# A transformer layer on one core: GpSimd's cost in the planner, head layout, fillers and the closing halves

## The chip, the cores and the metric

The kernel runs on one core of one Trainium2 chip. The metric is the device time of the whole program in microseconds (us); less is better. Five engines work from queues of their own, each strictly in its order: TensorE (PE, with its weight loads shown apart as PEld), VectorE (DVE), ScalarE (ACT), GpSimd (POOL) and SyncE (SP), which only issues transfers. They wait for each other on semaphores.

## The reference, cut to what matters

```python
xn = layernorm(x)                                  # x: 1 x 2048 x 128, f32
q, k, v = split(xn @ w_attn + b_attn)              # 16 heads of 8
scores = q @ k.T * 8 ** -0.5 + mask                # mask: -log(1 + delta) for keys AFTER the query, -inf before it
attn = softmax(scores) @ v
ffn = fp4(silu(fp4(xn) @ fp4(w_gate).T) * (fp4(xn) @ fp4(w_up).T)) @ fp4(w_down).T   # 352 wide
out = x + attn @ w_proj + b_proj + ffn
```

`fp4` quantizes blocks of 16 numbers and multiplies back. A query looks at itself and at the keys after it. Because the mask is minus a logarithm, exp(score + mask) = exp(score) / (1 + delta): the kernel multiplies the exponentials by a table of inverse distances, `dist`. This multiplication is called weighing here.

## The kernel before, in words

The 2048 queries are cut into four groups of 512 (`GROUPS = [3, 2, 0, 1]`) and the 16 heads into four quadruples. A group and a quadruple make a unit: 16 units. Each unit is walked twice. In the first walk (`max`) TensorE makes scores with queries on the partitions (L1425, with a triangle added at L1428) and VectorE takes the row maximum (L1240, 640 instructions). The maxima go back as three extra rows of the query operand, so that the second walk has them subtracted by the matmul itself. In the second walk (`st`), for each block of 128 keys and each head, TensorE makes the transposed scores (L1449, L1452), ScalarE the exponential (L1049), and then the exponentials are weighed and written into `ring`, eight slots of two heads each. A pair of heads is weighed either by GpSimd in one instruction over both heads (L895), after ScalarE has put the exponentials into the slot, or by VectorE in two instructions (L1267), which read PSUM and write the slot. A slot is `[P, GQ, 2]`: the two heads are interleaved, so VectorE writes every second number, and TensorE reads every second one. A step of four heads (two pairs) then goes through `pv` (L1467: the weighed values times V, four heads side by side on TensorE, accumulated in bank 7). There are 160 steps, 320 pairs, 640 heads. A slot is free again when the `pv` of its step is done, so `st` can be four steps ahead of `pv`.

After a unit's last step, ScalarE copies bank 7 out (`evac`, L1074), TensorE transposes it (`close`, L1475), and VectorE divides by the sums (`norm`, L1280 and L1281). After four units come a transpose (`turn`, L1483), ScalarE's copy with the bias (L1068), `project` (L1490), and VectorE's `add` into `xin` (L1292); SyncE stores the group (L795). The feed-forward part is cut into 16 tiles of 128 tokens and mixed in at fixed amounts of `st` work.

The order of every engine's queue is computed when the kernel is built, by `plan()`: a list scheduler that walks the four engines with a cost for each item. GpSimd's weighing costs `POOL_START + 2 * n * POOL_COL` there. The planner also decides, pair by pair, who weighs: VectorE if GpSimd's backlog, summed by the same cost, is above a bound.

```python
POOL_COL, POOL_START = 2.04, 220
POOL_QUEUE, LAST_QUEUE = 3800, 1500
behind = max(clock["POOL"], now) + waiting["POOL"] - now
pair_vec[p] = behind > (LAST_QUEUE if work["max"] == total else POOL_QUEUE)
```

`lead_at` says how far the maxima must be ahead of the second walk; VectorE puts a maximum ahead of a weighing only below that line. The same planner assigns the seven PSUM banks, and `bank_free_for` turns what held a bank before into a wait.

`FILL = 200` fillers (`warm`, L1310: a transpose of the identity into bank 7) have the lowest rank on TensorE and fill its gaps at the start. The first `pv`, which writes the same bank, is planned only after the last of them.

Of the kernel before, what the change touches and what calls it, by code (L numbers as in the profile page):

```python
# [12 lines left out]
P = 128  # L13
# [59 lines left out]
POOL_COL, POOL_START = 2.04, 220  # L73
# [4 lines left out]
def plan():  # L78
# [190 lines left out]
    bank_of, prior = {}, {}  # L269
    holder = [None] * BANKS  # L270
# [38 lines left out]
    def rank(engine, item, level, now):  # L309

        kind = item[0]
        if engine == "PE":
            free = len(free_banks(now))
            if kind in ("pv", "hT", "down", "warm"):
                return level
            if kind == "gu":
                return level if free >= 3 else None
            if kind == "max":
                ahead = issued["max"] - issued["maxed"]
                if ahead >= MAX_AHEAD or free < 2:  # L320
                    return None
                return 4 if ahead < 2 else 7
            if kind == "st":
                if issued["st"] - issued["exp"] >= EXP_AHEAD or issued["vec"] >= VEC_AHEAD or free < 2:
                    return None
                if item[1] // 2 >= SLOTS and ("PE", ("pv", (item[1] // 2 - SLOTS) // 2)) not in seen:
                    return None
                return 4.5
            return level if free >= 1 else None
        if engine == "DVE":  # L330
            if kind == "max":
                return 4 if work["max"] < lead_at(work["st"]) else 7
            if kind == "fp4" and item[2] == 2 and len(free_banks(now)) < HELD_FREE:
                return None
            return 5 if kind == "weigh" else level
        return level

    def take(engine, head, now):
# [7 lines left out]
        if engine == "PE" and kind not in ("pv", "hT", "down", "warm"):  # L346
            for o in [("gate", item[1]), ("up", item[1])] if kind == "gu" else [item]:
                b = min(free_banks(now), key=lambda k: (released(holder[k]) if holder[k] else 0, k))
                bank_of[o], prior[o], holder[b] = b, holder[b], o
# [6 lines left out]
        if engine == "ACT" and kind == "st":  # L356
# [62 lines left out]
    while True:  # L419
        busy = [e for e in queues if any(left[e].get(k, 0) < len(q) for k, q in queues[e].items())]  # L420
# [36 lines left out]
def build(nc, x, w_attn, b_attn, w_proj, b_proj, w_gate, w_up, w_down, out):  # L457
# [22 lines left out]
    with ExitStack() as ctx:  # L480
# [203 lines left out]

        def weights(d, n):
# [47 lines left out]
        def _(sp):  # L733
# [48 lines left out]
            for o in orders["SP"]:  # L782
# [8 lines left out]
                if o[0] == "out":  # L791
                    gi, g = o[1], GROUPS[o[1]]
                    sp.wait_ge(fin_ready, gi + 1)
                    sp.wait_ge(down_used, TPG * (gi + 1))
                    sp.dma_start(out_t[:, TPG * g:TPG * (g + 1), :],  # L795
                                 xin[:, TPG * g:TPG * (g + 1), :]).then_inc(stored, 16)
            sp.wait_ge(stored, 16 * NG)
# [123 lines left out]
        def _(act):  # L921
# [11 lines left out]
            for o in orders["ACT"]:  # L933
# [103 lines left out]
                if o[0] == "st":  # L1037
# [11 lines left out]
                    a_.activation(scores if pair_vec[p] else slot(p)[:, 0:n, e % 2], scores,  # L1049
# [11 lines left out]
                if o[0] == "turn":  # L1061
                    g = o[1]
                    act.wait_ge(attT_psum, g + 1)
# [4 lines left out]
                    a_.activation(attT, bank(*o), ACT.Identity, bias=bv[:]).then_inc(attT_ready, 1)  # L1068
                if o[0] == "evac":
# [4 lines left out]
                    a_.activation(osb[:, u % 2], psum[:, OUT_BANK, :], ACT.Identity).then_inc(o_ready, 1)  # L1074
# [3 lines left out]
        def _(vec):  # L1078
# [85 lines left out]
            for o in orders["DVE"]:  # L1164
# [93 lines left out]
                if o[0] == "weigh":  # L1258
# [8 lines left out]
                    v_.tensor_tensor(slot(p)[:, 0:n, e % 2], bank("st", e)[:, 0:n], weights(d, n),  # L1267
                                     ALU.mult).then_inc(weighed_vec, 1)
                if o[0] == "norm":
                    u = o[1]  # L1270
                    g, hq, _ = parts_of(u)
                    vec.wait_ge(oT_psum, u + 1)
                    if u >= NQ and hq == 0:
                        vec.wait_ge(attT_psum, u // NQ)
                    o4 = bank("close", u).rearrange("p (t j e) -> p t j e", t=TPG, j=4)
# [4 lines left out]
                    seq(v_.reciprocal(rz[:], o4[:, :, :, HD]))  # L1280
                    v_.tensor_tensor(att[:, :, 32 * hq:32 * hq + 32].rearrange("p t (j d) -> p t j d", d=HD),  # L1281
                                     o4[:, :, :, 0:HD],
                                     rz[:].rearrange("p t (j o) -> p t j o", o=1).to_broadcast([P, TPG, 4, HD]),
                                     ALU.mult).then_inc(att_ready, 1)
                if o[0] == "add":
                    g = GROUPS[o[1]]
                    res = xin[:, TPG * g:TPG * (g + 1), :]
                    vec.wait_ge(proj_psum, o[1] + 1)
                    if before(o, "sum") > 0:
                        vec.wait_ge(down_used, before(o, "sum"))  # L1290
                    projected = bank("project", o[1]).rearrange("p (t d) -> p t d", d=D)
                    v_.tensor_tensor(res, projected, res,  # L1292
                                     ALU.add).then_inc(fin_ready, 1)
# [3 lines left out]
        def _(pe):  # L1297
# [10 lines left out]
            for o in orders["PE"]:  # L1308
# [146 lines left out]
                if o[0] == "pv":  # L1455
# [9 lines left out]
                    for j in range(4):  # L1465
                        h = 4 * hq + j
                        ins = mm(psum[32 * j:32 * j + 32, OUT_BANK, 0:n], vaug[:, b, VC * h:VC * h + 32],  # L1467
                                 slot(2 * s + j // 2)[:, 0:n, j % 2], start=(b == NT - 1), stop=(b == TPG * g))
                    ins.then_inc(pv_done, 1)
                if o[0] == "close":  # L1470
                    u = o[1]
                    bank_free(*o)
                    pe.wait_ge(o_ready, u + 1)
                    for a in range(TPG):
                        ins = nc.tensor.transpose(bank(*o)[:, P * a:P * (a + 1)],  # L1475
                                                  osb[:, u % 2, P * a:P * (a + 1)], identf[:])
                    ins.then_inc(oT_psum, 1)
                if o[0] == "turn":
                    g = o[1]
                    bank_free(*o)  # L1480
                    pe.wait_ge(att_ready, 4 * g + 4)
                    for a in range(TPG):
                        ins = nc.tensor.transpose(bank(*o)[:, P * a:P * (a + 1)], att[:, a], identf[:])  # L1483
                    ins.then_inc(attT_psum, 1)
                if o[0] == "project":
                    g = o[1]
                    bank_free(*o)
                    pe.wait_ge(attT_ready, g + 1)
                    for a in range(TPG):
                        ins = mm(bank(*o)[:, P * a:P * (a + 1)], attT[:, P * a:P * (a + 1)], wp[:],  # L1490
                                 start=True, stop=True)
                    ins.then_inc(proj_psum, 1)
# [26 lines left out]
```

## Time and profile before

| | |
|---|---|
| median of 3 runs | 599.66 us (597.81 to 599.75) |
| the profiled execution: its time / its span | 599.36 us / 597.6 us |
| granted TensorE clock | 0.997 of full |
| TensorE, VectorE, GpSimd, ScalarE busy | 562.5, 547.1, 503.2, 409.3 us |
| weighings on GpSimd (pairs) / on VectorE (heads) | 223 / 194 |

Busy is the union of an engine's instructions. TensorE's matmuls are pipelined and their ends modelled, so its share overstates how close it is to its rate. The time has 1.8 us that lie outside the span.

### The profile page before, as it was taken

What the parts mean: (1) busy time and instruction counts of PE and PEld (TensorE: products, weight loads), DVE (VectorE), ACT (ScalarE), POOL (GpSimd) and SP (SyncE); (2) the same over time, 40 slices, a digit from 0 to 9 for tenths busy, and PEclk for the clock granted to TensorE, in tenths of its full rate; (3) what the DMA queues carried; (4) which work ended last, traced back from release to release, by engine and by line L of the source; (5) the groups of instructions that cost most, each with busy time, mean ns of one, the idle gap of its engine ahead of it and who ended that gap; (6) DMA issues with size and microseconds to landing.
All of it is one profiled execution on the core that took longest, in us unless ns stands there. A gap on an engine that the chain in (4) does not pass through costs nothing.

```text
span 597.6 us, 11270 instructions
## 1 busy us (share of the span) xinstructions
PE 562.5 (94%) x3791; PEld 247.5 (41%) x3791; DVE 547.1 (92%) x1165; ACT 409.3 (68%) x868; POOL 503.2 (84%) x409
## 2 busy tenths in 40 slices
PE   5999999999899999999999999999999998999995
PEld 4677844544343434333333333342344343343322
DVE  5999989998999899999999999999998989999672
ACT  4668486675665567766776676767666767677793
POOL 7378888797998889798999989897988889798773
PEclk9999999999998999999999999999999999999999
DMA  7434344010000001000000000000000000000000
GB/s 203 103 104 113 110 99 108 2 74 8 1 3 1 2 1 60 39 1 2 1 1 1 20 1 2 1 2 2 1 2 19 2 0 2 2 0 2 2 2 18
DMA packets 14832, 16.66 MB, mean 28 GB/s; under 512 B 1639, under 2 KB 14216, under 8 KB 14360
## 3 DMA queue, kind: packets, MB, share of 16 engines
q1 hardware_dynamic: 14240, 15.70, 9.5%
q8 instruction: 30, 0.49, 0.3%
q10 hardware_dynamic: 536, 0.26, 0.2%
q14 instruction: 26, 0.21, 0.1%
HBM read 11.75 MB, written 4.01 MB: 26 GB/s over the span
## 4 chain that ended last, share of the span: by engine, by line
PE 53%; DVE 27%; issue 7%; ACT 7%; POOL 5%; POOLq 0%; ACTq 0%; DVEq 0%
PE psum L1467 14%; DVE mxp L1240 13%; PE psum L1425 13%; PE psum L1449 10%; DVE ring L1267 4%; PE psum L1310 3%; POOL ring L895 3%; PE psum L1381 2%; ACT ring L1049 2%; PE psum L1400 2%; PE psum L1428 2%; PE psum L1383 1%; PE psum L1452 1%; DVE psum L1222 1%; DVE xw L1218 1%
## 5 line engine op out<-in xcount | busy, mean ns | idle before, releaser
L895 POOL TENSOR_TENSOR ring<-ring,dist 128x1024 f32<-128x1024 f32 (+3 forms) x223 | 398.6, 1815 | 51.6 <-ACT ring L1049 50.8
L1240 DVE TENSOR_REDUCE mxp<-psum 128x1 f32<-128x512 f32 (+3 forms) x640 | 354.7, 598 | 16.6 <-PE psum L1425 13.9
L1049 ACT ACTIVATE ring<-psum 128x512 f32<-128x512 f32 (+3 forms) x446 | 221.8, 557 | 93.5 <-PE psum L1452 46.8
L1425 PE MATMUL psum<-kop,qop 96*128 96x512 bf16 (+3 forms) x640 | 198.4, 352 | 7.2 <-DVE mxp L1240 3.7
L1449 PE MATMUL psum<-qop,kop 128*128 128x512 bf16 (+3 forms) x640 | 191.2, 349 | 7.4 <-DVE mxp L1240 2.8
L1467 PE MATMUL psum<-ring,vaug 128*32 128x512 f32 (+3 forms) x1280 | 155.3, 556 | 2.5 <-POOL ring L895 1.9
L1267 DVE TENSOR_TENSOR ring<-psum,dist 128x512 f32<-128x512 f32 (+3 forms) x194 | 115.1, 620 | 12.0 <-ACT psum L1049 11.4
L1049 ACT ACTIVATE psum<-psum 128x512 f32<-128x512 f32 (+3 forms) x194 | 99.7, 545 | 31.7 <-PE psum L1449 19.0
L1425 PEld LDWEIGHTS psum<-kop,qop 96*128 96x128 bf16 x640 | 56.5, 97 | 134.6 <-DVE mxp L1240 45.5
L1449 PEld LDWEIGHTS psum<-qop,kop 128*128 128x128 bf16 x640 | 59.3, 97 | 83.6 <-DVE mxp L1240 19.7
L1428 PE MATMUL psum<-tri_q,identb 128*128 128x128 bf16 x256 | 55.9, 220 | 0.0
L1452 PE MATMUL psum<-tri_k,identb 128*128 128x128 bf16 x256 | 52.5, 219 | 0.0
L1467 PEld LDWEIGHTS psum<-ring,vaug 128*32 128x32 f32 x1280 | 25.8, 108 | 48.7 <-issue 47.1
L1428 PEld LDWEIGHTS psum<-tri_q,identb 128*128 128x128 bf16 x256 | 25.2, 99 | 13.5 <-issue 1.9
L1310 PE MATMUL psum<-identf 128*128 128x128 f32 x200 | 30.8, 274 | 0.0
L1452 PEld LDWEIGHTS psum<-tri_k,identb 128*128 128x128 bf16 x256 | 25.1, 98 | 7.7 <-issue 0.3
L1310 PEld LDWEIGHTS psum<-identf 128*128 128x128 f32 x200 | 22.4, 141 | 3.5 <-issue 0.5
L1017 ACT ACTIVATE xw<-psum 128x352 f32<-128x352 f32 x16 | 7.4, 464 | 17.1 <-PE psum L1383 17.1
L911 POOL TENSOR_TENSOR xw<-xw 128x352 f32<-128x352 f32 x16 | 15.1, 942 | 3.6 <-DVE xw L1226 3.5
L1056 ACT ACTIVATE mrow<-psum 12x512 bf16<-12x512 bf16 x16 | 9.3, 581 | 11.9 <-PE psum L1436 11.9
L1400 PE MATMUL psum<-wdT,hT 128*128 128x128 f32 (+1 forms) x96 | 15.2, 296 | 1.7 <-ACT hT L1035 1.6
L913 POOL TENSOR_TENSOR xw<-xw 128x352 f32<-128x352 f32 x16 | 15.0, 938 | 1.3
(134 smaller groups left out, 467.9 us busy)
## 6 DMA issues: line engine op xcount, KB each, us to landing
parts_dram<-qpart SPq DMA_DIRECT2D x18, 128.0 KB, 3.4
kop<-parts_dram SPq DMA_DIRECT2D x6, 384.0 KB
qop<-parts_dram SPq DMA_DIRECT2D x6, 384.0 KB
xin<-_attn_hidden_states_dram SPq DMA_DIRECT2D x4, 256.0 KB, 5.0
ring<-inv_dram SPq DMA_DIRECT2D x1, 1024.0 KB, 5.1
out_dram<-xin SPq DMA_DIRECT2D x4, 256.0 KB, 2.3
qop<-parts_dram SPq DMA_DIRECT2D x3, 288.0 KB
kop<-parts_dram SPq DMA_DIRECT2D x3, 288.0 KB
```

Of the source, the lines that this page charges most:

```text
L895: g_.tensor_tensor(slot(p)[:, 0:n], slot(p)[:, 0:n], both, ALU.mult).then_inc(weighed_pool, 1)
L911: g_.tensor_tensor(v, v, c, ALU.add).then_inc(hq_seq, 1)
L1049: a_.activation(scores if pair_vec[p] else slot(p)[:, 0:n, e % 2], scores, ACT.Exp, scale=SCALE).then_inc(exp_done, 1)
L1240: v_.tensor_reduce(mxp[:, u % 2, 4 * a + j, c - g:c - g + 1], bank(*o)[:, 0:n], AX_X, ALU.max).then_inc(max_used, 1)
L1267: v_.tensor_tensor(slot(p)[:, 0:n, e % 2], bank("st", e)[:, 0:n], weights(d, n), ALU.mult).then_inc(weighed_vec, 1)
L1310: nc.tensor.transpose(psum[:, OUT_BANK, 0:P], identf[:], identf[:])
L1400: ins = mm(down_of(i), hT[0:k, i % 2, m], wdT[0:k, m], start=(m == 0), stop=(m == 2))
L1425: ins = mm(bank(*o)[:, 0:n], qop[0:K_MAX, u // NQ % 2, h, P * a:P * (a + 1)], kop[0:K_MAX, h, k0:k0 + n], start=True, stop=(c != g))
L1428: ins = mm(bank(*o)[:, 0:P], identb[:], tri_q[:], start=False, stop=True)
L1449: ins = mm(bank(*o)[:, 0:n], kop[0:K_ST, h, P * b:P * (b + 1)], qop[0:K_ST, u // NQ % 2, h, 0:n], start=True, stop=(d >= TPG))
L1452: ins = mm(bank(*o)[:, P * d:P * (d + 1)], identb[:], tri_k[:], start=False, stop=True)
L1467: ins = mm(psum[32 * j:32 * j + 32, OUT_BANK, 0:n], vaug[:, b, VC * h:VC * h + 32], slot(2 * s + j // 2)[:, 0:n, j % 2], start=(b == NT - ...
```

## The change

Four edits.

1. `plan()` walks GpSimd's weighings with 1.906 ns for each number and 140 ns for the start, in place of 2.04 and 220. All four orders, the choice of who weighs each pair and the banks follow from it.
2. A pair weighed by VectorE lies in its slot with one head after the other (`weighted`), so VectorE writes and TensorE reads adjacent numbers. GpSimd's pairs stay interleaved.
3. The first `pv` no longer waits for the last filler; once it has been planned no filler is planned, and those that are left are dropped.
4. The last unit's `evac`, `close`, `norm`, and the last group's `turn`, `project`, `add` and store are issued in two halves, tiles 2 and 3 first, then 0 and 1, each half with its own semaphore count; the matmul stages use a second bank for the second half. The last step's four heads are always weighed by VectorE.

```diff
-POOL_COL, POOL_START = 2.04, 220
+POOL_COL, POOL_START = 1.906, 140
...
-        if s == 0 and FILL:
-            needs.append(("PE", ("warm", FILL - 1)))
...
+    halved = {("close", len(units) - 1), ("turn", NG - 1), ("project", NG - 1)}
...
+            if kind == "warm" and ("PE", ("pv", 0)) in seen:
+                return None
...
-            return level if free >= 1 else None
+            return level if free >= 1 + (item in halved) else None
...
-                pair_vec[p] = behind > (LAST_QUEUE if work["max"] == total else POOL_QUEUE)
+                pair_vec[p] = behind > (LAST_QUEUE if work["max"] == total else POOL_QUEUE) or e >= 4 * len(steps) - 4
...
+        def weighted(p, j, n):
+            if pair_vec[p]:
+                return slot(p).rearrange("p n j -> p (n j)")[:, GQ * j:GQ * j + n]
+            return slot(p)[:, 0:n, j]
+        def shares(ends):
+            return ((2, 4), (0, 2)) if ends else ((0, TPG),)
+        def share_bank(part, *o):
+            return bank(*o, 1) if part else bank(*o)
...
-                    v_.tensor_tensor(slot(p)[:, 0:n, e % 2], bank("st", e)[:, 0:n], weights(d, n),
+                    v_.tensor_tensor(weighted(p, e % 2, n), bank("st", e)[:, 0:n], weights(d, n),
...
-                    a_.activation(osb[:, u % 2], psum[:, OUT_BANK, :], ACT.Identity).then_inc(o_ready, 1)
+                    for t0, t1 in shares(u == len(units) - 1):
+                        a_.activation(osb[:, u % 2, P * t0:P * t1], psum[:, OUT_BANK, P * t0:P * t1],
+                                      ACT.Identity).then_inc(o_ready, 1)
...
-                                 slot(2 * s + j // 2)[:, 0:n, j % 2], start=(b == NT - 1), stop=(b == TPG * g))
+                                 weighted(2 * s + j // 2, j % 2, n), start=(b == NT - 1), stop=(b == TPG * g))
...
+                    for part, (t0, t1) in enumerate(shares(g == NG - 1)):
+                        if part:
+                            bank_free(*o, 1)
+                        pe.wait_ge(attT_ready, g + 1 + part)
+                        for a in range(t0, t1):
+                            ins = mm(share_bank(part, *o)[:, P * a:P * (a + 1)], attT[:, P * a:P * (a + 1)], wp[:],
+                                     start=True, stop=True)
+                        ins.then_inc(proj_psum, 1)
```

`close`, `norm`, `turn`, `add` and the store are cut in the same way.

## Rows read from the trace of the kernel before

**Rows 1.** The page, part 1: busy time, share of the span, instructions.

```profile
PE 562.5 (94%) x3791; PEld 247.5 (41%) x3791; DVE 547.1 (92%) x1165; ACT 409.3 (68%) x868; POOL 503.2 (84%) x409
```

**Rows 2.** Busy us by stage: length, PE, PEld, DVE, ACT, POOL, clock, DMA share, GB/s.

```profile
62.00:552.00 490.00, 470.67 (x3128) 193.60 (x3126) 467.55 (x964) 337.39 (x730) 433.23 (x302) 1.00 0.06 17
552.00:590.00 38.00, 34.32 (x259) 11.40 (x255) 23.76 (x46) 30.98 (x70) 28.61 (x22) 1.00 0.01 1
```

**Rows 3.** The same stage, GpSimd's weighing instructions (line 895) alone.

```profile
62.00:552.00 490.00, 373.05 (x208) 1.00 0.06 17
```

**Rows 4.** Part 4 of the page: the chain that ended last, by engine.

```profile
PE 53%; DVE 27%; issue 7%; ACT 7%; POOL 5%; POOLq 0%; ACTq 0%; DVEq 0%
```

**Rows 5.** Groups by line and shape: count, busy us, mean ns, idle before.

```profile
L895 POOL TENSOR_TENSOR ring<-ring,dist 128x1024 f32<-128x1024 f32 x153 | 323.5, 2139 | 46.6 <-ACT ring L1049 45.9
...
L1467 PE MATMUL psum<-ring,vaug 128*32 128x512 f32 x896 | 123.9, 623 | 2.0 <-POOL ring L895 1.5 <-issue 0.3
L1267 DVE TENSOR_TENSOR ring<-psum,dist 128x512 f32<-128x512 f32 x142 | 93.0, 681 | 10.4 <-ACT psum L1049 10.0
...
L895 POOL TENSOR_TENSOR ring<-ring,dist 128x256 f32<-128x256 f32 x28 | 18.4, 674 | 4.0 <-ACT ring L1049 3.9
...
L1210 DVE TENSOR_TENSOR xw<-psum,xw 128x352 f32<-128x352 f32 x16 | 8.2, 514 | 0.0
...
L1267 DVE TENSOR_TENSOR ring<-psum,dist 128x256 f32<-128x256 f32 x20 | 7.7, 414 | 0.7 <-ACT psum L1049 0.5
...
L1049 ACT ACTIVATE psum<-psum 128x256 f32<-128x256 f32 x20 | 7.1, 403 | 2.9 <-PE psum L1452 2.9
...
L1352 PE MATMUL psum<-ring,flip 128*128 128x512 f32 x8 | 4.3, 619 | 0.0
```

**Rows 6.** Timeline of GpSimd (start, length): the first weighing, and five in a row.

```profile
61.83 2.13 POOL L895 TENSOR_TENSOR ring<-ring,dist 128x1024 f32<-128x1024 f32 x1
...
309.13 10.54 POOL L895 TENSOR_TENSOR ring<-ring,dist 128x1024 f32<-128x1024 f32 x5
```

**Rows 7.** Timeline of VectorE: the last maximum, and four weighings in a row.

```profile
551.72 0.69 DVE L1240 TENSOR_REDUCE mxp<-psum 128x1 f32<-128x512 f32 x1
...
572.67 2.48 DVE L1267 TENSOR_TENSOR ring<-psum,dist 128x512 f32<-128x512 f32 x4 [0.84 <-ACT psum L1049]
```

**Rows 8.** Timeline around the first `pv` step, fillers included.

```profile
66.79 0.43 ACT L1049 ACTIVATE psum<-psum 128x128 f32<-128x128 f32 x2 [0.33 <-PE psum L1452]
...
73.39 0.71 PE L1310 MATMUL psum<-identf 128*128 128x128 f32 x5
...
74.58 1.10 PE L1467 MATMUL psum<-ring,vaug 128*32 128x512 f32 x8
...
76.10 1.13 ACT L1049 ACTIVATE ring<-psum 128x512 f32<-128x512 f32 x2 [2.84 <-PE psum L1452]
```

**Rows 9.** Timeline of the end, from the last exponentials to the store.

```profile
587.04 0.62 ACT L1049 ACTIVATE ring<-psum 128x128 f32<-128x128 f32 x3 [0.42 <-PE psum L1452]
...
587.40 1.31 POOL L895 TENSOR_TENSOR ring<-ring,dist 128x256 f32<-128x256 f32 x2 [0.24 <-ACT ring L1049]
...
588.85 0.43 PE L1467 MATMUL psum<-ring,vaug 128*32 128x128 f32 x8 [0.21 <-POOL ring L895]
589.35 0.60 ACT L1074 ACTIVATE osb<-psum 128x512 f32<-128x512 f32 x1 [1.69 <-PE psum L1467]
...
590.09 0.63 PE L1475 MATMUL psum<-identf,osb 128*128 128x128 f32 x4 [0.80 <-ACT osb L1074]
590.75 0.26 DVE L1280 RECIPROCAL rz<-psum 128x16 f32<-128x16 f32 x1 [3.70 <-PE psum L1475]
...
592.15 0.69 ACT L1068 ACTIVATE xw<-psum,bv 128x512 f32<-128x512 f32 x1 [2.20 <-PE psum L1483]
...
592.98 1.13 PE L1490 MATMUL psum<-wp,xw 128*128 128x128 f32 x8 [0.87 <-ACT xw L1068]
...
594.86 0.38 SPq L795 DMA_DIRECT2D out_dram<-xin  x1
```

More of the change, by code:

```diff
@@ L419, in plan @@
     while True:
-        busy = [e for e in queues if any(left[e].get(k, 0) < len(q) for k, q in queues[e].items())]
+        busy = [e for e in queues if any(k != "warm" and left[e].get(k, 0) < len(q) for k, q in queues[e].items())]
         if not busy:
@@ L1279, in _ @@
                         vec.wait_ge(att_ready, u)
[L1280 to L1284, printed above, removed]
+                    for part, (t0, t1) in enumerate(shares(u == len(units) - 1)):
+                        o4 = share_bank(part, "close", u).rearrange("p (t j e) -> p t j e", t=TPG, j=4)
+                        vec.wait_ge(oT_psum, u + 1 + part)
+                        seq(v_.reciprocal(rz[:, t0:t1], o4[:, t0:t1, :, HD]))
+                        v_.tensor_tensor(att[:, t0:t1, 32 * hq:32 * hq + 32].rearrange("p t (j d) -> p t j d", d=HD),
+                                         o4[:, t0:t1, :, 0:HD],
+                                         rz[:, t0:t1].rearrange("p t (j o) -> p t j o", o=1).to_broadcast(
+                                             [P, t1 - t0, 4, HD]), ALU.mult).then_inc(att_ready, 1)
                 if o[0] == "add":
                     g = GROUPS[o[1]]
-                    res = xin[:, TPG * g:TPG * (g + 1), :]
-                    vec.wait_ge(proj_psum, o[1] + 1)
                     if before(o, "sum") > 0:
                         vec.wait_ge(down_used, before(o, "sum"))
-                    projected = bank("project", o[1]).rearrange("p (t d) -> p t d", d=D)
-                    v_.tensor_tensor(res, projected, res,
-                                     ALU.add).then_inc(fin_ready, 1)
+                    for part, (t0, t1) in enumerate(shares(o[1] == NG - 1)):
+                        vec.wait_ge(proj_psum, o[1] + 1 + part)
+                        res = xin[:, TPG * g + t0:TPG * g + t1, :]
+                        projected = share_bank(part, "project", o[1]).rearrange("p (t d) -> p t d", d=D)
+                        v_.tensor_tensor(res, projected[:, t0:t1], res, ALU.add).then_inc(fin_ready, 1)
         @block.tensor
@@ L1472, in _ @@
                     bank_free(*o)
[L1473 to L1477, printed above, removed]
+                    for part, (t0, t1) in enumerate(shares(u == len(units) - 1)):
+                        if part:
+                            bank_free(*o, 1)
+                        pe.wait_ge(o_ready, u + 1 + part)
+                        for a in range(t0, t1):
+                            ins = nc.tensor.transpose(share_bank(part, *o)[:, P * a:P * (a + 1)],
+                                                      osb[:, u % 2, P * a:P * (a + 1)], identf[:])
+                        ins.then_inc(oT_psum, 1)
                 if o[0] == "turn":
@@ L1480, in _ @@
                     bank_free(*o)
[L1481 to L1484, printed above, removed]
+                    for part, (t0, t1) in enumerate(shares(g == NG - 1)):
+                        if part:
+                            bank_free(*o, 1)
+                        pe.wait_ge(att_ready, 4 * g + 4 + part)
+                        for a in range(t0, t1):
+                            ins = nc.tensor.transpose(share_bank(part, *o)[:, P * a:P * (a + 1)], att[:, a], identf[:])
+                        ins.then_inc(attT_psum, 1)
                 if o[0] == "project":
@@ L1487, in _ @@
                     bank_free(*o)
[L1488 to L1492, printed above, removed]
+                    for part, (t0, t1) in enumerate(shares(g == NG - 1)):
+                        if part:
+                            bank_free(*o, 1)
+                        pe.wait_ge(attT_ready, g + 1 + part)
+                        for a in range(t0, t1):
+                            ins = mm(share_bank(part, *o)[:, P * a:P * (a + 1)], attT[:, P * a:P * (a + 1)], wp[:],
+                                     start=True, stop=True)
+                        ins.then_inc(proj_psum, 1)
 _INS = ['L0_attn_hidden_states', 'L0_attn_w_attn', 'L0_attn_b_attn', 'L0_attn_w_proj', 'L0_attn_b_proj',
```

20 lines of the change are left out of this document (10 added, 10 removed).

## The prediction, made before the kernel ran

> **What bounds the kernel now.** I read the page's busy line first [rows 1]: TensorE and VectorE are both above 90%, GpSimd is at 84%, ScalarE at 68%. That is an average over stages, so I cut the span where the work changes: GpSimd's first weighing starts at 61.8 us [rows 6] and the last maximum at 551.7 us [rows 7]. From 62 to 552 us, in 490 us, VectorE is busy 467.6 us: it stands still for 22.4 us only. TensorE shows 470.7 us, but its ends are modelled; GpSimd shows 433.2 us and is the one of the three with room [rows 2]. After 552 us no maxima are left, VectorE is busy 23.8 of 38 us, and TensorE (34.3) and ScalarE (31.0) carry the rest. So the reader should see two stages: a long one in which VectorE has almost no gap, and a short one in which it doesn't matter.
>
> The chain that ended last [rows 4] gives TensorE 53% and VectorE 27%. These two hand work to each other through seven banks, and a chain picks one of two engines that are both nearly full. I read VectorE as the one with less room, and the chain as a warning that TensorE stands close behind it.
>
> Last, who waits for whom: the idle column of the groups [rows 5]. GpSimd's weighings of 1024 numbers wait 45.9 us for ScalarE, and TensorE's `pv` of 512 columns waits for GpSimd 1.5 us in all. GpSimd is thus starved, not late. Why it starves is in the lengths. A weighing of 1024 numbers takes 2139 ns and one of 256 takes 674 ns [rows 5]: 1.908 ns for each number, 185 ns fixed. Five in a row take 10.54 us [rows 6], so a next one starts (10.54 - 2.14) / 4 = 2.10 us after the one before, some 42 ns less than its length. The old planner gives it 220 + 2.04 x 1024 = 2309 ns, the new one 140 + 1.906 x 1024 = 2092 ns. The old one is 0.21 us too high, and the new one right to 8 ns. The planner sends pairs to VectorE when GpSimd's backlog looks long; it looks longer than it is, and the real GpSimd runs dry.
>
> **Edit 1, GpSimd's cost.** From 62 to 552 us it weighs 208 pairs in 373.05 us [rows 3]: 1794 ns each, which is (1794 - 185) / 1.908 = 843 numbers, a pitch of 1.75 us. The old cost exceeds the pitch by 220 + 2.04 x 843 - 1750 = 190 ns, times 208: 39.5 us of room, near to the 45.9 us of waiting. With the right cost this room is filled with pairs taken from VectorE. On VectorE four heads in a row of 512 columns take 2.48 us [rows 7], a pitch of (2.48 - 0.68) / 3 = 0.60 us; the lengths of 681 and 414 ns for 512 and 256 columns [rows 5] give 1.043 ns a column, so a head of 421 columns has a pitch of 0.505 us and a pair costs 1.01 us. If VectorE bounds the stage, N pairs moved shorten it by 1.01 N, which takes the same from GpSimd's room: 1.75 N = 39.5 - 1.01 N, so N = 14.3 pairs and a gain of 14.5 us at most. GpSimd would then do some 237 pairs, VectorE some 165 heads.
>
> At least it is worth nothing: if TensorE bounds the stage, the time freed on VectorE is idle. TensorE's 19.3 us without work in this stage [rows 2] and its share of the chain [rows 4] say that a part is lost, since with three engines full each head-of-queue wait has less behind it to hide it. I take three quarters, 10.9 us, nearer to the upper end because VectorE's gap (22.4 us) is as small as TensorE's while TensorE's busy time is the overstated one. Both ends stay in the range. ScalarE writes 28 heads more into `ring` and as many fewer back to PSUM: the same exponentials with another target, on an engine that is busy 337 of 490 us in this stage [rows 2], so nothing.
>
> Here a rule of the Trainium skill speaks against the change. What rows show: a pair costs 1.75 us on GpSimd and 1.01 us on VectorE, so 14.3 pairs moved add 0.74 x 14.3 = 10.6 us to the sum of the engines' work. The skill's "GPSIMD Engine Reference", section "Engine selection", sends elementwise work on tiles to VectorE, as GpSimd is about twice as slow with two inputs. The trace agrees on the ratio (1.7); by the rule alone the time would rise, by the rows it falls as long as GpSimd has idle time. What would make the rule right is a rival below.
>
> **Edit 2, the layout.** VectorE: a contiguous product of PSUM and SBUF takes 514 ns for 352 columns [rows 5]. The interleaved form by its two lengths would take 681 - 160 x 1.043 = 514 ns. Nothing gained. TensorE: f32 operands read contiguously take 619 ns for 512 columns, and the interleaved ones of `pv` 623 ns [rows 5]. The gain is between 0 and 4 ns on the matmuls that read VectorE's pairs, under 400 of 1280: at most 1.6 us of TensorE's time, and I take 0. A loss has no row; the two layouts in one step could at worst differ by the same few ns.
>
> **Edit 3, the fillers.** The ring is full when the exponentials of step 3 end at 67.2 us. The next start at 76.1 us, after the first `pv` at 74.58 us, and TensorE spends the time between on fillers, up to 74.1 us [rows 8]. Without the wait `pv` can start when its pairs are weighed, near 67 us, and the second walk goes on some 7 us earlier. But VectorE used the time for maxima that have to be made anyway, and GpSimd for the fp4 pieces. The stage's sum of work doesn't change; what is gained is only GpSimd's and VectorE's idle time there. The bounds are 0 and 3 us (7 us of earlier start by the share 1.01 / 2.76 at which GpSimd's time becomes time of the stage, 2.6 us). I take 0.6 us. If the cover is gone, that is if `pv` in fact starts before VectorE has maxima to do, the whole 7 us would be idle: excluded, as VectorE's queue is full in this stretch. The granted clock is 1.00 there [rows 2], and real work follows the fillers, so I put no price on the clock.
>
> **Edit 4, the end.** Before: `evac` starts at 589.35, the store is issued at 594.86 [rows 9]: 5.51 us of seven stages in series, each whole. In halves the second half sets the end. ScalarE: 0.40 us for 256 columns [rows 5], the second one 0.28 us behind (three of 128 columns take 0.62 [rows 9] and two 0.43 [rows 8], a pitch of 0.19; for 256 I take 0.28, between that and the whole length): done at 0.68. Gap to TensorE 0.14 (590.09 - 589.95), two of four transposes 0.40 (of 0.63): 1.22. VectorE has its first half's reciprocal and product to do until about 1.46, then its second, 0.24 + 0.25: 1.95. Gap 0.14 and transposes 0.40: 2.49. ScalarE after 0.04, 0.40: 2.93. Gap 0.14, four of eight matmuls 0.65 (of 1.13): 3.72. The sum 0.41 and two gaps of 0.03 (590.75 - 590.72): 4.19. So 1.3 us are saved. The store's second half lands from 128 KB rather than 256 KB, 0 to 0.2 us, I take 0.1. The last step's weighing: GpSimd's two take 1.31 us from 587.40 to 588.71 and `pv` starts at 588.85 [rows 9]. On VectorE the four heads follow the exponentials, which end at 587.66, by one product of about 0.28 us: `pv` near 588.2, 0.5 us earlier, at worst 0 because TensorE's wider steps before it run until about then. Together 1.9 us, between 1.2 and 2.2. The halves add no waits for anything queued behind them: nothing is.
>
> **Sum.** 10.9 + 0 + 0.6 + 1.9 = 13.4 us. From the profiled execution's own 599.36 us: 586.0 us. That execution is 0.3 us under the median, so the same holds for the median: 586.
>
> **Rivals.** A: the room on GpSimd isn't turned into time. Either the planner's backlog bound leaves the number of pairs where it is, or TensorE bounds the long stage and VectorE's freed time is idle. For it: the chain [rows 4] and TensorE's 470.7 us. Against it: VectorE's gap is as small. Left is 0 to 5 us of edit 1 and 1.2 to 2.5 us of the others: 592 to 598 us, with 595 in the middle.
>
> B, on the other side: `pv` at the head of TensorE's queue starts waiting for GpSimd. Before, GpSimd ran 0.19 us ahead of plan at every pair, so that `pv` found its pairs ready (1.5 us of waits) [rows 5]. Now this slack is gone: a weighing is over 2139 ns after its start, the plan says 2092 + 60. Each wait holds up maxima and scores queued behind `pv`, and so VectorE. It eats the 13.4 us when it is 84 ns at each of the 160 steps; at 0.12 us, that is 19 us, the time is 605. Against it: five weighings keep a pitch of 2.10 us while VectorE is nearly full [rows 2, 6], so GpSimd is as regular as the plan has it, and the plan keeps up to three maxima ready in front of VectorE (`MAX_AHEAD`).
>
> C: it gains more, since GpSimd's and VectorE's remaining idle time shrinks too and the earlier `pv` gives its 2.6 us: 14.5 + 2.6 + 2.2 = 19.3, and up to 3 us from a better fit of all orders: 577 to 580.
>
> **How the numbers follow.** My forecast, 580 to 592 us: 0.60. A: 0.16. B: 0.16. C: 0.08. A measurement of this kernel tells about 0.3%, 1.8 us, from no change: 597.9 to 601.5 is "the same". A reaches it with 0.04, where edit 1 gives nothing and the rest little; B with 0.05, where the waits of `pv` are some 75 to 95 ns. Faster: 0.60 + 0.12 + 0.08 = 0.80; same: 0.09; slower: 0.11 of B. The range goes from 578 to 599: below it lies a part of C (0.03), above it nearly all of B (0.15). The likeliest case's own is 580 to 592.
>
> **What would show it.** Edit 1: L895 235 to 240 times in place of 223, L1267 fewer; its wait for ScalarE (45.9 us at 1024 numbers) under 25 us; GpSimd over 88% busy; the last maximum near 540 us instead of 552. If the maximum ends at 550 with VectorE's gaps grown, it is A; if `pv`'s wait for GpSimd is over 10 us, B. Edit 2: L1267 still 681 ns at 512 columns. Edit 3: the first `pv` near 67 us and fewer than 150 fillers. Edit 4: from `evac` to the last store's issue 4.2 us. The forecast fails if the new orders place `pv` or the banks worse than now, which no row of the old order can show.

## The result, and the profile after

The changed kernel takes 599.59 us (median of 20 runs), the one before 598.72 us in the same calls: a ratio of 1.0028, 95% interval 1.0015 to 1.0041. The ratio, which is taken over the undisturbed runs, makes 1.7 us (the medians alone lie 0.9 us apart). 586 us were forecast; the result lies in the middle of what was called "the same" (597.9 to 601.5) and 0.6 us above the upper end of the range, 599.

The page after: busy time, the chain, and the groups of the weighings and maxima (GpSimd's line is 910 now, `pv`'s 1487, VectorE's products 1286, the maxima 1259).

```profile
PE 558.4 (93%) x3760; PEld 244.8 (41%) x3760; DVE 539.4 (90%) x1154; ACT 409.0 (68%) x870; POOL 522.2 (87%) x416
...
PE 53%; POOL 24%; ACT 9%; DVE 8%; issue 4%; POOLq 0%; ACTq 0%; DVEq 0%
...
L910 POOL TENSOR_TENSOR ring<-ring,dist 128x1024 f32<-128x1024 f32 (+3 forms) x230 | 418.6, 1848 | 37.0 <-ACT ring L1064 36.3
L1259 DVE TENSOR_REDUCE mxp<-psum 128x1 f32<-128x512 f32 (+3 forms) x640 | 355.4, 603 | 18.8 <-PE psum L1445 10.7
...
L1487 PE MATMUL psum<-ring,vaug 128*32 128x512 f32 (+3 forms) x1280 | 156.7, 554 | 11.3 <-POOL ring L910 9.7
L1286 DVE TENSOR_TENSOR ring<-psum,dist 128x512 f32<-128x512 f32 (+3 forms) x180 | 103.0, 602 | 16.5 <-ACT psum L1064 16.2
```

The stages after, with the columns of [rows 2], and then GpSimd's and `pv`'s waits (us in all, how many, the longest):

```profile
62.00:552.00 490.00, 465.28 (x3090) 190.13 (x3088) 460.32 (x949) 335.31 (x728) 448.45 (x311) 1.00 0.06 17
552.00:590.00 38.00, 34.22 (x254) 11.46 (x258) 22.90 (x47) 31.89 (x72) 32.47 (x20) 1.00 0.00 1
590.00:598.00 8.00, 3.75 (x32) 2.47 (x20) 1.62 (x6) 1.50 (x4) 0.00 (x0) 0.73 0.11 33
```

```profile
POOL ring L910 <- ACT ring L1064: 36.3, 38, 2.4
...
PE psum L1487 <- POOL ring L910: 9.7, 24, 1.2
```

Set beside [rows 1, 2, 4, 5]: seven pairs have moved to GpSimd (230 against 223), VectorE has 7.7 us less to do, and GpSimd is busy 19 us longer. In the long stage VectorE now idles 29.7 us instead of 22.4. The chain passes through GpSimd with 24% in place of 5%, and through VectorE with 8% in place of 27%. `pv` waits 9.7 us for GpSimd. The last maximum starts near 538.7 us, 13 us earlier than before:

```profile
537.26 2.08 DVE L1259 TENSOR_REDUCE mxp<-psum 128x1 f32<-128x512 f32 x4
...
543.87 1.29 DVE L1286 TENSOR_TENSOR ring<-psum,dist 128x512 f32<-128x512 f32 x2 [1.30 <-ACT psum L1064]
```

And yet the second walk ends no earlier: the last `evac` starts at 590.55 us, where it started at 589.35. VectorE got rid of 7.2 us of work in the long stage and idles 7.2 us longer there. The end after:

```profile
587.19 2.27 POOL L910 TENSOR_TENSOR ring<-ring,dist 128x512 f32<-128x512 f32 x2 [0.46 <-ACT ring L1064]
...
588.38 0.89 DVE L1286 TENSOR_TENSOR ring<-psum,dist 128x128 f32<-128x128 f32 x4 [2.02 <-ACT psum L1064]
...
589.61 0.88 PE L1487 MATMUL psum<-ring,vaug 128*32 128x256 f32 x16 [1.24 <-POOL ring L910]
590.55 0.66 ACT L1092 ACTIVATE osb<-psum 128x256 f32<-128x256 f32 x2 [1.70 <-PE psum L1487]
...
592.21 0.78 PE L1509 MATMUL psum<-identf,xw 128*128 128x128 f32 x4 [0.44 <-DVE xw L1301]
...
593.33 1.78 PE L1519 MATMUL psum<-wp,xw 128*128 128x128 f32 x8 [0.34 <-ACT xw L1084]
594.37 0.42 DVE L1313 TENSOR_TENSOR xin<-psum,xin 128x256 f32<-128x256 f32 x1 [1.94 <-PE psum L1519]
594.87 1.11 SPq L810 DMA_DIRECT2D out_dram<-xin  x2
595.15 0.42 DVE L1313 TENSOR_TENSOR xin<-psum,xin 128x256 f32<-128x256 f32 x1 [0.36 <-PE psum L1519]
```

From `evac` to the end of the last sum are 595.57 - 590.55 = 5.02 us, where it was 594.83 - 589.35 = 5.48 us before [rows 9]; `project` alone takes 1.78 us where it took 1.13. The windows of one microsecond show why (third column from the end: the granted clock):

```profile
592.00:593.00 1.00, 0.78 (x4) 1.00 0.00 0
593.00:594.00 1.00, 0.67 (x4) 0.81 0.00 0
594.00:595.00 1.00, 1.00 (x6) 0.50 0.00 0
```

The clock fell from 2.4 to 1.2 GHz at 593.6 us, inside `project`. TensorE had stood still for 1.24 us before the last `pv` and then between the short stages of the closing; whether that is why it fell is looked at with e17 below.

### The profile page after: what moved, and what is told of

It reads as the page before. It is cut to its first block, busy times and chain, and to the rows that moved or that the text cites. A ratio compares the mean times of both kernels' runs of the same rounds, so it can differ in the third digit from the quotient of the medians.

```text
span 597.8 us, 11210 instructions
## 1 busy us (share of the span) xinstructions
PE 558.4 (93%) x3760; PEld 244.8 (41%) x3760; DVE 539.4 (90%) x1154; ACT 409.0 (68%) x870; POOL 522.2 (87%) x416
## 4 chain that ended last, share of the span: by engine, by line
PE 53%; POOL 24%; ACT 9%; DVE 8%; issue 4%; POOLq 0%; ACTq 0%; DVEq 0%
POOL ring L910 18%; PE psum L1487 15%; PE psum L1445 12%; PE psum L1469 9%; DVE mxp L1259 4%; ACT ring L1064 3%; PE psum L1420 2%; PE psum L1330 2%; PE psum L1401 2%; POOL xw L928 2%; POOL xw L926 2%; POOL xw L930 1%; PE psum L1448 1%; PE psum L1403 1%; PE psum L1409 1%
## 5 line engine op out<-in xcount | busy, mean ns | idle before, releaser
L910 POOL TENSOR_TENSOR ring<-ring,dist 128x1024 f32<-128x1024 f32 (+3 forms) x230 | 418.6, 1848 | 37.0 <-ACT ring L1064 36.3
L1064 ACT ACTIVATE ring<-psum 128x512 f32<-128x512 f32 (+3 forms) x460 | 230.4, 568 | 106.7 <-PE psum L1472 50.5
L1487 PE MATMUL psum<-ring,vaug 128*32 128x512 f32 (+3 forms) x1280 | 156.7, 554 | 11.3 <-POOL ring L910 9.7
L1286 DVE TENSOR_TENSOR ring<-psum,dist 128x512 f32<-128x512 f32 (+3 forms) x180 | 103.0, 602 | 16.5 <-ACT psum L1064 16.2
L1064 ACT ACTIVATE psum<-psum 128x512 f32<-128x512 f32 (+3 forms) x180 | 88.8, 530 | 27.3 <-PE psum L1472 13.6
L1330 PE MATMUL psum<-identf 128*128 128x128 f32 x169 | 26.2, 275 | 0.0
L1330 PEld LDWEIGHTS psum<-identf 128*128 128x128 f32 x169 | 18.8, 141 | 2.7 <-issue 0.5
L1420 PEld LDWEIGHTS psum<-wdT,hT 128*128 128x128 f32 (+1 forms) x96 | 11.9, 191 | 7.1 <-ACT hT L1050 7.0
```

What stands on the lines that cost most here:

```text
L910: g_.tensor_tensor(slot(p)[:, 0:n], slot(p)[:, 0:n], both, ALU.mult).then_inc(weighed_pool, 1)
L1064: a_.activation(scores if pair_vec[p] else weighted(p, e % 2, n), scores, ACT.Exp, scale=SCALE).then_inc(exp_done, 1)
L1286: v_.tensor_tensor(weighted(p, e % 2, n), bank("st", e)[:, 0:n], weights(d, n), ALU.mult).then_inc(weighed_vec, 1)
L1330: nc.tensor.transpose(psum[:, OUT_BANK, 0:P], identf[:], identf[:])
L1420: ins = mm(down_of(i), hT[0:k, i % 2, m], wdT[0:k, m], start=(m == 0), stop=(m == 2))
```

## The experiments

Five theories are set against each other. S: edit 1 loses its gain because the exact cost leaves GpSimd's results no lead, and TensorE's order waits for them (rival B of the prediction). T: another edit eats what edit 1 gains. After the first four runs, P: TensorE and ScalarE, the chain of the second walk, bound the kernel (rival A), and G: GpSimd does. After the next eight, N: any new order costs some time, since the order before is a good one among many like it.

All times are ratios to the kernel before on the same chip, with 95% intervals; 0.1% is 0.6 us.

### Each edit alone

```diff
e1_cost     -POOL_COL, POOL_START = 2.04, 220
            +POOL_COL, POOL_START = 1.906, 140
e2_layout   +            if pair_vec[p]:
            +                return slot(p).rearrange("p n j -> p (n j)")[:, GQ * j:GQ * j + n]
e3_fillers  -            needs.append(("PE", ("warm", FILL - 1)))
            +            if kind == "warm" and ("PE", ("pv", 0)) in seen:
            +                return None
e4_closing  +    halved = {("close", len(units) - 1), ("turn", NG - 1), ("project", NG - 1)}
            +    pair_vec[p] = behind > (...) or e >= 4 * len(steps) - 4
```

e1_cost: 

> Edit 1 alone, GpSimd's cost of 1.906 ns and 140 ns in the kernel before. Theory S (the gain of edit 1 is lost again because the exact cost leaves GpSimd's results no lead, and TensorE's order waits for them): within 3 us of before, the pairs on GpSimd above 223 and the wait of the values' matmuls for GpSimd at 5 us or more against 1.9 us. Rival T (another edit eats what edit 1 gains): 586 to 590 us.

e2_layout: 

> Edit 2 alone, VectorE's heads contiguous; the orders are those of before. Theory S: within 0.5 us of before, the product of 512 columns still 681 ns and the values' matmuls of 512 columns still 623 ns. Rival T: at least 3 us slower, with one of the two lengths up by 10 ns or more.

e3_fillers: 

> Edit 3 alone, the first values' step free of the last fillers. Theory S: within 2 us of before, the first values' matmul near 68 us instead of 74.6. Rival T: 3 us slower or more, since all orders behind it are others.

e4_closing: 

> Edit 4 alone, the closing in halves and the last four heads on VectorE, with the costs, the layout and the fillers of before. Theory S: 0.3 to 1.5 us faster. Rival T: slower than before by 1 us or more, because the granted clock falls in the closing and the matmuls there take twice their time.

| alone | ratio | interval |
|---|---|---|
| edit 1, cost | 1.0043 | 1.0026 to 1.0060 |
| edit 2, layout | 1.0013 | 0.9998 to 1.0028 |
| edit 3, fillers | 1.0041 | 1.0024 to 1.0058 |
| edit 4, closing | 0.9973 | 0.9960 to 0.9987 |

Edit 1, the one with 10.9 us of the forecast's 13.4, costs 2.6 us by itself, so rival T is out. It did what it says: 236 pairs on GpSimd, where the forecast worked out 237, and the waits grew as theory S has it. VectorE has 11.3 us less to do, GpSimd 23.7 us more. From the page and the waits of edit 1 alone:

```profile
PE 555.9 (93%) x3740; PEld 249.4 (42%) x3791; DVE 535.8 (89%) x1139; ACT 408.7 (68%) x868; POOL 526.9 (88%) x422
...
PE 47%; POOL 28%; ACT 11%; DVE 7%; issue 5%; another core or an unknown queue 1%; ACTq 0%; POOLq 0%; DVEq 0%
```

```profile
POOL ring L895 <- ACT ring L1049: 32.5, 34, 3.0
...
PE psum L1467 <- POOL ring L895: 11.1, 23, 1.2
```

The layout's lengths are 682 ns for the product and 622 ns for the values' matmul of 512 columns, as before within 1 ns; its ratio is not clear of 1. Edit 3 alone is 2.5 us slower, which neither expectation has (within 2 us, or 3 us and more); its first `pv` starts at 70.70 us, and the first unit's `evac` 3.6 us earlier than before, a lead that is gone by the seventh unit. The closing in halves is the only edit that pays. It is also the only one of the three that touch `plan()` which keeps the orders of before, but for who weighs the last pairs. Here the closing runs before the clock falls, and is 4.37 us long (587.79 to 592.16), 1.1 us shorter than before:

```profile
586.17 1.56 PE L1485 MATMUL psum<-ring,vaug 128*32 128x384 f32 x24
...
587.79 0.66 ACT L1090 ACTIVATE osb<-psum 128x256 f32<-128x256 f32 x2 [1.27 <-PE psum L1485]
...
590.57 1.13 PE L1517 MATMUL psum<-wp,xw 128*128 128x128 f32 x8 [0.34 <-ACT xw L1082]
591.36 0.80 DVE L1311 TENSOR_TENSOR xin<-psum,xin 128x256 f32<-128x256 f32 x2 [1.69 <-PE psum L1517]
```

### Which engine's work is worth time

The orders are kept as they are, and one engine at a time gets less to do; each of these kernels leaves out a part of the work:

```diff
GpSimd    +                    n = n * 9 // 10
ScalarE   +                    if e >= 160:
          +                        n = n * 85 // 100
TensorE   +                    if b < NT - 1:
          +                        n = n * 3 // 4
VectorE   -  ...bank(*o)[:, 0:n],
          +  ...bank(*o)[:, 0:n if c == g else n * 4 // 5],
```

On the changed kernel:

e5_gpsimd_less: 

> The changed kernel with its orders kept, but GpSimd weighs only 9 of 10 columns of each of its pairs, which takes some 37 us of work from GpSimd (0.16 us a pair). The last tenth stays unweighed. Theory G (GpSimd is the bound after edit 1, since TensorE's order waits for its results): 10 us faster or more. Theory P (the second walk's chain over TensorE and ScalarE is the bound): under 4 us faster.

e6_tensor_less: 

> The changed kernel with its orders kept, but the values' matmuls take three quarters of their columns from the second step of each unit on, some 25 us less work on TensorE. A quarter of the sums is left out. Theory P: 8 us faster or more. Theory G: under 4 us faster.

e7_scalar_less: 

> The changed kernel with its orders kept, but from the 160th head on ScalarE takes the exponential of 85% of the columns, some 25 us less work on ScalarE; the others keep old or raw values. Theory P with ScalarE as its longer part: 5 us faster or more. Theory G: under 3 us faster.

e8_vector_less: 

> The changed kernel with its orders kept, but VectorE's maxima off the diagonal read four fifths of their columns, some 41 us less work on VectorE; the maxima are those of the part read. The forecast's reading, that VectorE bounds the long stage, wants 15 us or more. Theories G and P: under 5 us.

On the kernel before:

e9_before_vector_less: 

> The kernel before with its orders kept and VectorE's maxima off the diagonal over four fifths of their columns, some 34 us less work on VectorE; the maxima are those of the part read. If VectorE bounded the long stage before, as the forecast read it, 10 us faster or more. If TensorE's chain bounds it there too (theory P), under 4 us.

e10_before_gpsimd_less: 

> The kernel before with its orders kept and GpSimd weighing 9 of 10 columns of its pairs, some 36 us less work on GpSimd; the last tenth stays unweighed. Since it was starved there: under 2 us faster. If it gives 8 us, as it did on the changed kernel, its lead over the plan wasn't what protected the kernel before.

e11_before_tensor_less: 

> The kernel before with its orders kept and the values' matmuls over three quarters of their columns from the second step of each unit on, some 24 us less work on TensorE; a quarter of the sums is left out. Theory P (TensorE bounds both kernels): 8 us faster or more, as on the changed one. If VectorE bounded it before: under 4 us.

e12_before_scalar_less: 

> The kernel before with its orders kept and ScalarE's exponentials over 85% of the columns from the 160th head on, some 27 us less work on ScalarE; the others keep old or raw values. Theory P: 2 to 6 us faster. If VectorE bounded it before: under 2 us.

| less work on | busy us less | before: ratio (interval), us | changed: ratio (interval), us against its own 1.0028 |
|---|---|---|---|
| VectorE | 34 | 0.9898 (0.9862 to 0.9934), -6.1 | 1.0016 (0.9996 to 1.0035), -0.7 |
| GpSimd | 37 | 0.9997 (0.9984 to 1.0010), -0.2 | 0.9879 (0.9855 to 0.9903), -8.9 |
| TensorE | 24 | 0.9823 (0.9801 to 0.9844), -10.6 | 0.9848 (0.9821 to 0.9875), -10.8 |
| ScalarE | 26 to 27 | 0.9977 (0.9964 to 0.9991), -1.4 | 0.9962 (0.9947 to 0.9977), -4.0 |

The busy times are differences of the pages' first lines, TensorE's that of the changed pair, whose records are equally complete. For one microsecond of work TensorE gives 0.44 us in both kernels. VectorE gave 0.18 us before (0.12 to 0.24 by its interval) and gives 0.02 us now; GpSimd gave nothing and now gives 0.24 us. With GpSimd relieved in the changed kernel (e5), TensorE waits 9.3 us less for it: `pv` 2.7 us in place of 9.7, and L1409, which reads what GpSimd leaves of the feed-forward tiles, 2.4 in place of 4.7. That is near the 8.9 us gained.

```profile
POOL ring L911 <- ACT ring L1065: 59.7, 53, 3.5
...
PE psum L1488 <- POOL ring L911: 2.7, 6, 1.0
```

What a microsecond is worth was measured on VectorE's maxima, on GpSimd's weighings and on `pv`. Edit 1 takes weighings from VectorE, not maxima, and no run prices those by themselves. Two of these pages' busy lines show how the table is read, VectorE relieved in the kernel before and then in the changed one:

```profile
PE 552.0 (93%) x3740; PEld 247.4 (42%) x3791; DVE 513.2 (87%) x1165; ACT 408.0 (69%) x868; POOL 502.7 (85%) x409
```

```profile
PE 555.0 (93%) x3760; PEld 243.7 (41%) x3760; DVE 505.1 (85%) x1154; ACT 408.4 (68%) x870; POOL 521.8 (87%) x416
```

VectorE is at 87% and 85%, yet the first run is 6.1 us faster and the second only 0.7 us. The forecast's reading, "VectorE bounds the long stage", wanted 10 and 15 us. Theory P's limit for e8 holds, while for e9 neither expectation does: VectorE had some weight before, but a small one. Theory P is also borne out by e6 and e11 (8 us or more). In e5 (8.9 us, where G wanted 10 or more and P under 4) and e7 (4.0 us, between G's 3 and P's 5) neither is, and e12 gives 1.4 us where P wanted 2 to 6. So no single engine bounds the changed kernel: TensorE weighs most and GpSimd next.

### Lost lead, a wrong price for TensorE, or just another order

```diff
e13  -POOL_COL, POOL_START = 2.04, 220
     +POOL_COL, POOL_START = 2.04, 221
e14  +POOL_COL, POOL_START = 2.04, 225
e15  e1, and  -        add("POOL", item, took, 0, needs, **more)
              +        add("POOL", item, took, 212, needs, **more)
e16  e4, and  -PV_SWITCH = 310
              +PV_SWITCH = 600
```

e13_neighbour_221: 

> The kernel before with GpSimd's start planned at 221 ns instead of 220: a cost that hardly differs, but 49 of 320 pairs change their engine and a third of TensorE's queue its place. If edit 1's 2.5 us are the price of moving 13 pairs, this one is within 1 us of before. If any new order costs as much (theory N, the kernel before is a lucky order), it is 1 to 4 us slower.

e14_neighbour_225: 

> The same with 225 ns, another order with the same load. Theory N: 1 to 4 us slower than before. Else within 1 us.

e15_cost_lead: 

> Edit 1 alone, but the planner lets each of GpSimd's results be seen 212 ns later, which gives back the lead and keeps the exact load (238 pairs). If the lost lead is what edit 1 costs (theory S), 3 us faster than edit 1 alone or more, and TensorE's wait for GpSimd is back under 4 us. If TensorE's own work bounds the kernel (theory P), within 1.5 us of edit 1 alone.

e16_closing_pv: 

> Edit 4 alone with the values' step planned at 600 columns of switch instead of 310, which makes it 1.12 us for 512 columns, as the trace has it. If TensorE's under-priced step is what makes the orders bad (theory P in its strong form), 2 to 6 us faster than edit 4 alone. If only its work counts and not its price in the plan: within 2 us of it.

| | ratio | interval | pairs on GpSimd | `pv` waits for GpSimd, us |
|---|---|---|---|---|
| e13, 221 ns | 1.0093 | 1.0073 to 1.0112 | 222 | 2.4 |
| e14, 225 ns | 1.0043 | 1.0027 to 1.0058 | 224 | 4.6 |
| e15, edit 1 with the lead back | 1.0048 | 1.0030 to 1.0065 | 238 | 5.1 |
| e16, edit 4 with the dearer `pv` | 1.0094 | 1.0075 to 1.0114 | 219 | 4.6 |

Theory S is not borne out, and not refuted either. e15 halves the wait of `pv`, from 11.1 to 5.1 us (not to under 4, as expected), and the time stays that of edit 1 alone. But e15 is a new order itself, and GpSimd keeps its place in the chain: 27%, with 28% in edit 1 alone and 5% before. And e5 says that with the order kept, GpSimd's lateness does cost time. How much of edit 1's 2.6 us is GpSimd's lateness therefore stays open. The chain and the two waits of e15:

```profile
PE 45%; POOL 27%; ACT 9%; DVE 9%; issue 5%; DMA 3%; SPq 1%; ACTq 0%; POOLq 0%; DVEq 0%
...
POOL ring L895 <- ACT ring L1049: 31.5, 39, 2.5
...
PE psum L1467 <- POOL ring L895: 5.1, 14, 0.9
```

The strong form of P falls: planned with TensorE's true price the order is 7 us worse than edit 4's. Theory N stands: 5 ns more in a cost (e14), with every engine but TensorE, whose records differ, busy within 1 us of before, make the kernel 2.6 us slower, and one nanosecond more (e13) 5.6 us, 1.6 us beyond what I expected of it. All eight kernels of this document that have new orders (the changed one, e1, e3, e13 to e16, e18) are slower than before, by 0.22% to 0.94%. The page and waits of e13, beside [rows 1, 5]; GpSimd is busy 5.0 us less and VectorE 3.1 us more:

```profile
PE 559.5 (93%) x3741; PEld 248.0 (41%) x3791; DVE 550.2 (91%) x1167; ACT 410.0 (68%) x868; POOL 498.2 (83%) x408
```

```profile
POOL ring L895 <- ACT ring L1049: 57.3, 53, 4.3
...
PE psum L1467 <- POOL ring L895: 2.4, 7, 0.5
```

By the prices above, these differences would not make 1 us; it is 0.9% slower all the same. Up to the tenth unit the two run alike (`evac` at 344.7 us before and 344.9 in e13); then e13 falls behind, by 8.0 us at the fourteenth unit and 5.2 us at the last `evac`. Another 0.9 us is the clock: `project` takes 2.04 us there in place of 1.13. It takes 2.04 us also in e1, e3, e14 and e15, and no execution of e1, e13 or e14 has a mean clock above 0.995, while most of the kernel before have 1.0. So some 0.9 of the 2.6 us that e1 and e14 each lose is the closing's clock.

### The clock in the closing, and the filler edit beside the others

```diff
e17  +                if o == ("pv", len(steps) - 2):
     +                    bank_free("close", len(units) - 1)
     +                    hold(8, last_bank)
     +                if o == ("close", len(units) - 1):
     +                    hold(4, last_bank)
     +                if o in (("turn", NG - 1), ("project", NG - 1)):
     +                    hold(3, psum[:, OUT_BANK, 0:P])
e18  the changed kernel without edit 3
```

`hold` issues transposes of the identity.

e17_hold_clock: 

> The changed kernel with fillers on TensorE in the closing: eight before the last but one values' step, four before the close, three before the turn and three before the projection, into banks that are free there. If the fall of the clock costs the closing, the four matmuls of the projection take 1.1 us again in place of 1.8 and the kernel is 0.5 to 1 us faster than the changed one. Rival: the clock falls all the same and the fillers only stand in the way, 0 to 0.7 us slower.

e18_no_filler_edit: 

> The changed kernel without edit 3: the first values' step waits for 200 fillers as before. The sum of the single edits says 2.5 + 0.8 - 1.6 = 1.7 us over before, where the changed kernel itself is 1.7 us over it. If effects of orders don't add up (theory N), it lies anywhere between 3 us faster and 4 us slower than before.

```profile
591.40 0.66 ACT L1092 ACTIVATE osb<-psum 128x256 f32<-128x256 f32 x2 [1.71 <-PE psum L1500]
...
593.67 0.49 PE L1332 MATMUL psum<-identf 128*128 128x128 f32 x3
...
594.18 1.13 PE L1532 MATMUL psum<-wp,xw 128*128 128x128 f32 x8
594.97 0.80 DVE L1313 TENSOR_TENSOR xin<-psum,xin 128x256 f32<-128x256 f32 x2 [1.69 <-PE psum L1532]
```

e17 is at 1.0027 (1.0012 to 1.0043). In its profiled execution `project` takes 1.13 us again, and from `evac` to the last sum it is 595.77 - 591.40 = 4.37 us against 5.02. The whole doesn't show it; 0.65 us is below what the interval can tell. Nor is it shown that the transposes did it. e8 has the order and the gaps of the changed kernel, no transposes, and keeps the clock; e13 stands still for only 0.23 us before its last `pv` and loses it. The last `pv` and `project` of e8, then of e13:

```profile
588.64 0.88 PE L1487 MATMUL psum<-ring,vaug 128*32 128x256 f32 x16 [1.24 <-POOL ring L910]
...
592.36 1.13 PE L1519 MATMUL psum<-wp,xw 128*128 128x128 f32 x8 [0.34 <-ACT xw L1084]
...
594.06 0.43 PE L1467 MATMUL psum<-ring,vaug 128*32 128x128 f32 x8 [0.23 <-POOL ring L895]
...
598.18 2.04 PE L1490 MATMUL psum<-wp,xw 128*128 128x128 f32 x8 [0.87 <-ACT xw L1068]
```

The changed kernel's own twenty executions differ too: the six fastest (598.75 to 598.99 us) have a mean clock of 0.999 or 1.0, the next five (599.30 to 599.61 us) 0.996 or 0.997.

e18 is at 1.0022 (1.0010 to 1.0035): edit 3 makes no difference that shows beside the others, though alone it costs 2.5 us. The single edits add up to +0.70%, the change as a whole costs 0.28%. With orders that all differ, the effects don't add.

The fastest kernel that computes the whole layer is edit 4 alone: at 0.9973 (0.9960 to 0.9987) it beats both.

## Why the prediction was wrong

**The step that failed** is in edit 1: "I take three quarters, 10.9 us, nearer to the upper end because VectorE's gap (22.4 us) is as small as TensorE's while TensorE's busy time is the overstated one." The number of pairs was right (236 in e1 for 237; the changed kernel, with the other edits, has 230), and VectorE's relief nearly so (11.3 us in e1 for 14.5). What was wrong is what this relief is worth. On the kernel before, 34 us less work on VectorE gave 6.1 us, a fifth and not three quarters. At that price 14.5 us of relief would have given 2.6 us, and e1's 11.3 us give 2.0, even if the added load on GpSimd had been free (an estimate: the price was measured on maxima, and edit 1 moves weighings). It isn't free: relieving GpSimd is worth 0.24 us for a microsecond in the changed kernel and nothing in the one before, so that its 13 pairs more, 23.7 us of work, can cost anything between 0 and 5.7 us. TensorE, which the chain had named with 53% [rows 4], has more than twice VectorE's weight. I set the chain aside for a comparison of two idle times, and a busy share of 95% turned out to say little on whether the engine sets the pace: the relief experiments give VectorE less than half of TensorE's weight at the same share.

**Rival A** had the mechanism: VectorE's freed time is idle (22.4 us of gaps became 29.7) while TensorE weighs most. Its price of 592 to 598 us failed since it had new orders at worst neutral. Its sign failed too: the last maximum came 13 us earlier and not at 550, so an early last maximum is no sign of a gain. **Rival B** saw `pv`'s waits come (9.7 us in 24 waits, near the 10 us it named) and priced them as the cost. e5 supports that in part: with the order kept, less work on GpSimd takes most of these waits away and gives 8.9 us. e15 has half the waits of e1 and is no faster, but in another order. So B's share is between nothing and all of what GpSimd's added load can cost, and stays open.

**What was missing** is the spread of orders, named in the last sentence of the prediction and given neither size nor chance. Two neighbours with nearly the same load are 0.43% and 0.93% slower than before. The kernel before is thus a good order among the nine seen here, and every edit here that re-plans came out 1.3 to 5.6 us behind it, the two neighbours 2.6 and 5.6 us, of which some 0.9 us is the clock in the closing. Edit 1 alone at +0.43% is no worse than these neighbours. The 4.6 us between its estimated gain of 2.0 and its measured loss of 2.6 are thus the clock in the closing (0.9 us), GpSimd's added load and the new order, and no run separates the last two. Whether the order of edit 1 is better than the average order cannot be told from two neighbours; that stays open, and so does what makes the order of before the better one.

**Edit 2** was right: nothing that is clear of noise. **Edit 3** was priced at 0.6 us: in the changed kernel `pv` starts at 68.6 us, for the forecast's 67, with 169 fillers rather than under 150; alone it is 2.5 us slower, within what the neighbours show, so the fillers themselves are not shown to cost anything. **Edit 4** was forecast at 1.9 us, and alone it gives 1.6 us (0.8 to 2.4). Its trace bears out the parts: the closing is 1.1 us shorter for the forecast's 1.3, what follows the last sum 0.3 us for 0.1 (a term that had no row), and the last unit, from the `evac` before it, 0.4 us for 0.5. (The two traces lie 3.0 us apart; 1.4 us of that arises between 177 and 205 us, where the orders are equal and the granted clock of the kernel before was 0.83 from 190 to 200 us.) In the changed kernel the closing is about 0.5 us shorter: "so I put no price on the clock" was said of the fillers and never asked of the closing, where the clock takes 0.65 us of the 1.1. And `pv` waits 1.24 us for GpSimd shortly before it, where the kernel before had 0.21.

The Trainium skill's rule ("GPSIMD Engine Reference", "Engine selection") that elementwise work belongs on VectorE came out on the right side: the time did not fall with the move, though no run here separates the rule from the spread of orders.

## What to carry to other kernels

Before work is moved off an engine, keep the orders and give that engine less to do, best in the instructions that are to move: one run tells what a microsecond on it is worth, and here it would have said 0.18 us and 0.44 us for two engines with nearly the same busy share. Do the same for the engine that is to take the work, in the changed order. Where an order is computed, run two or three neighbours first; a change that re-plans has to beat their spread and not only the kernel before. A planner that is made more exact in one cost isn't thereby better: GpSimd's exact cost (e1) and the dearer `pv` (e16) both gave slower kernels. That the old costs had been chosen together with their errors may be why, but no run shows it.

## What the runs showed of the hardware

The granted clock can fall inside the closing: at 593.6 us in the changed kernel's profiled execution, with `project` at 1.78 us instead of 1.13, and at 594.6 us in edit 1 alone, with 2.04. In edit 4 alone the closing ends at 592.2 us and the clock is still at 2.4 GHz. The gap before the last `pv` doesn't decide it: 1.24 us and no fall in e8, 0.23 us and a fall in e13. Executions of one kernel differ in it as well. What decides it is not shown.

An f32 operand at a stride of two numbers costs nothing that shows: VectorE's product of 512 columns takes 681 ns with it and 682 ns without, and the values' matmul 623 and 622 ns.
